# Boundary mask from two digit one-hots, decay matrices in pairs, and the last back turns and statistics placed in the attention loop's first bodies

## The reference, cut to what matters

```python
x = x + jnp.tanh(g_xattn[0]) * _L0_xattn_ref(_layernorm(x, axis=-1), ctx_2048, mask_BxS2_if0, ...)
x = x + jnp.tanh(g_ffn[0]) * _L0_ffn_ref(_layernorm(x, axis=-1), ...)
x = x + jnp.tanh(g_xattn[1]) * _L1_xattn_ref(ctx_2048, _layernorm(x, axis=-1), mask, mask, ...)
x = x + jnp.tanh(g_ffn[1]) * _L1_ffn_ref(_layernorm(x, axis=-1), ...)
```

```python
bidx = jnp.cumsum(patch_lens, axis=1) - 1
boundary_mask = boundary_mask.at[jnp.arange(bsz)[:, None], bidx].set(1)
...
_, s = jax.lax.associative_scan(comb, (a_b, u), axis=1)
plug = jnp.clip(jnp.cumsum(boundary_mask, axis=1) - 1, 0, plen - 1)
depool_out = depool[jnp.arange(bsz)[:, None], plug]
```

## Time and profile before

| | us |
|---|---|
| median of 3 runs | 769.09 (767.45 to 769.4) |
| the profiled execution | 770.5 |
| its span | 768.7 |

### The profile page before, as it was taken

The page is one execution under the profiler, slowest core; times in us unless marked ns, Lnnn a source line. Parts: engine busy times, 40 slices in busy tenths (PEclk is TensorE's granted clock), DMA queues, the critical chain, the costliest instruction groups (busy, mean ns, idle before and its releaser), DMA issues.

```text
span 768.7 us, 12459 instructions
## 1 busy us (share of the span) xinstructions
PE 703.1 (91%) x3826; PEld 491.1 (64%) x3826; DVE 518.5 (67%) x998; ACT 418.9 (54%) x1127; POOL 206.4 (27%) x278
## 2 busy tenths in 40 slices
PE   3788999999999996699999999999999986799996
PEld 1465655554544365588888888888888865456554
DVE  7576477666675376778887877788878787423423
ACT  1666655535545531565566566655665565345352
POOL 3555433310110031533322323233223220212120
PEclk9679999999999998799999999999999999899999
DMA  6621203810000022333334444333344330001112
GB/s 196 219 84 55 83 29 104 234 55 1 0 1 1 0 48 63 83 92 97 82 90 110 110 110 110 81 81 81 86 110 110 82 83 1 1 1 55 35 48 82
DMA packets 46021, 57.48 MB, mean 75 GB/s; under 512 B 14080, under 2 KB 24480, under 8 KB 45856
## 3 DMA queue, kind: packets, MB, share of 16 engines
q1 hardware_dynamic: 45984, 57.03, 27.4%
HBM read 27.52 MB, written 4.19 MB: 41 GB/s over the span
## 4 chain that ended last, share of the span: by engine, by line
PE 77%; ACT 9%; DVE 9%; issue 3%; POOL 0%; DMA 0%; DVEq 0%; ACTq 0%
PE bank L1037 11%; PE bank L1219 7%; ACT c_p L859 7%; PE bank L1292 7%; PE bank L1271 6%; PE bank L1049 5%; PE bank L1411 4%; PE bank L1285 4%; PE bank L1013 4%; PE bank L1258 4%; PE bank L1237 3%; PE bank L1017 3%; DVE c_nmx L1709 3%; PE bank L1402 2%; PE bank L1323 2%
## 5 line engine op out<-in xcount | busy, mean ns | idle before, releaser
L859 ACT ACTIVATE c_p<-bank,c_nmx 128x256 f32<-128x256 f32 x256 | 117.5, 487 | 42.9 <-DVE c_nmx L1709 42.9
L1722 DVE TENSOR_TENSOR c_p<-c_p,c_inv 128x1024 f32<-128x1024 f32 x64 | 91.6, 1432 | 1.1
L1037 PE MATMUL bank<-b_o,cw 128*128 128x512 f32 x192 | 90.8, 603 | 0.0
L1709 DVE TENSOR_REDUCE c_nmx<-bank 128x4 f32<-128x1024 f32 x64 | 75.3, 1219 | 19.9 <-PE bank L1258 19.9
L1271 PE MATMUL bank<-ident,c_p 128*128 128x128 f32 x512 | 65.2, 276 | 8.2 <-ACT c_p L859 8.2
L1271 PEld LDWEIGHTS bank<-ident,c_p 128*128 128x128 f32 x512 | 58.5, 143 | 16.0 <-ACT c_p L859 8.9
L945 ACT ACTIVATE d_h<-bank,b_col 128x512 f32<-128x512 f32 x64 | 39.6, 686 | 45.8 <-PE bank L1403 45.7
L1219 PE MATMUL bank<-c_ctxT,wsrcT 128*128 128x256 f32 x256 | 62.0, 387 | 1.4 <-ACT c_ctxT L835 1.4
L728 ACT ACTIVATE b_h<-bank,cb 128x512 f32<-128x512 f32 x48 | 33.0, 687 | 53.8 <-PE bank L1037 53.7
L1037 PEld LDWEIGHTS bank<-b_o,cw 128*128 128x128 f32 x192 | 34.2, 190 | 41.6 <-issue 41.2
L1729 DVE COPY c_pT<-bank 128x512 f32<-128x512 f32 x64 | 43.9, 686 | 23.8 <-PE bank L1271 23.8
(11 more groups left out here) (185 smaller groups left out, 1450.5 us busy)
## 6 DMA issues: line engine op xcount, KB each, us to landing
c_stack<-c_parts SPq DMA_DIRECT2D x192, 128.0 KB
a_ctx<-in_ctx SPq DMA_DIRECT2D x16, 512.0 KB, 3.4
c_ctx<-in_ctx SPq DMA_DIRECT2D x16, 512.0 KB, 3.5
out_x<-x_sb SPq DMA_DIRECT2D x8, 512.0 KB, 3.0
x_sb<-in_x SPq DMA_DIRECT2D x3, 1024.0 KB, 7.5
mask_b<-in_mask_BxS_fk SPq DMA_DIRECT2D x1, 2048.0 KB, 11.7
x_sb<-in_x SPq DMA_DIRECT2D x2, 512.0 KB, 7.4
wsrc_raw<-in_L_xattn_W_src SPq DMA_DIRECT2D x1, 1024.0 KB, 7.1
```

What stands on the lines that cost most here:

```text
L859: op = nc.scalar.activation(c_p[hg][:, tc, j, :], scores(tc)[:, j, :], ACT.Exp, bias=c_nmx[hg][:, tc, j:j + 1], accum_out=c_sum[hg][:, tc, ...
L1037: op = mm(bank[2 * u + h][:], cw1[:, c, h * P:(h + 1) * P], b_o[n % LANES][:, c, :], start=c == 0, stop=c == DK - 1)
L1709: v.tensor_reduce(c_nmx[hg][:, tc, :], scores(tc), AXIS.X, ALU.max, negate=True)\
L1722: v.tensor_tensor(pr, pr, c_inv[hg][:, :, js].unsqueeze(3).to_broadcast([P, TS, 2, S]), ALU.mult)\
```

## The change

The boundary position is split into a high and a low digit of base 16. Two VectorE instructions compare all 32 columns of positions with 16 digits, 32 small matmuls make, for each batch, a 16 x 16 table of hits, ACT takes its Sign, and 16 small transposes bring the tables back into rows of 256 in bank 1. Lags and decays are made for two batches at a time, over banks 0 to 3 and two `a_z` buffers, in rounds of 2, 1, 2, 2 and 1 pairs; `decay_a` of the last pair comes after the waits for the weights of stage B on ACT. ACT takes the gates and `squares_a(0)` ahead of the Sign and `winT`. At the junction of B and C, `back_b(6)` and `back_b(7)` with `x_b(6)` and `x_b(7)` go from ahead of the loop into body 0; `stats_b(4)` and `stats_b(5)` to the end of body 0, `stats_b(6)` and `stats_b(7)` to the end of body 1; `ones_c(1)` on GpSimd into body 0. `update_b(11, 1)` follows `v_c(0, 3)` at once.

```diff
-LAG_BANK = (1, 2, 3)
-LAGS = (range(0, 3), range(3, 6), range(6, 11), range(11, 16), ())
+LAGS = (range(0, 2), range(2, 3), range(3, 5), range(5, 7), range(7, 8))
+LO = 16
+HI = S // LO
...
-            iota_bf = sb("iota_bf", [P, S], BF16, st)
+            iota_lo = sb("iota_lo", [P, LO], I32, st)
...
-            boundT = sb("boundT", [P, TS, B], F32, st)
-            hit = [sb(f"hit{s}", [P, TS, S], BF16, st) for s in range(4)]
-            row_at = sb("row_at", [P, 2 * B - 1], BF16, st)
-            ends = sb("ends", [B, S], F32, st)
+            bound_i = sb("bound_i", [P, TS * B], I32, st)
+            bound_hi = sb("bound_hi", [P, TS * B], I32, st)
+            bound_lo = sb("bound_lo", [P, TS * B], I32, st)
+            hit_hi = sb("hit_hi", [P, TS * B, HI], BF16, st)
+            hit_lo = sb("hit_lo", [P, TS * B, LO], BF16, st)
...
-            a_z = [sb(f"a_z{s}", [P, QT], F32, st) for s in range(3)]
+            a_z = [sb(f"a_z{s}", [P, 2, QT], F32, st) for s in range(2)]
...
-            a_mT = [sb(f"a_mT{b}", [P, QT], F32, st) for b in range(B)]
+            a_mT = sb("a_mT", [P, B, QT], F32, st)
...
-            nc.gpsimd.iota(iota_bf[:], pattern=[[1, S]], base=0, channel_multiplier=0,
+            nc.gpsimd.iota(iota_lo[:], pattern=[[1, LO]], base=0, channel_multiplier=0,
...
-            nc.gpsimd.memset(row_at[:], 0.0).then_inc(s_zero, 1)
-            pool.wait_ge(s_zero, 2)
-            nc.gpsimd.memset(row_at[:, B - 1:B], 1.0).then_inc(s_const, 1)
...
+                if is_first(b):
+                    pool.wait_ge(c_xb, 2)
+                    ones_c(1, b_x2, NG)
...
+                if isinstance(b, int) and b < 2:
+                    stats_b(NG // 2 + 2 * b)
+                    stats_b(NG // 2 + 2 * b + 1)
...
-            for n in range(NG // 2, NG):
-                stats_b(n)
-            ones_c(1, b_next, 2 * NG)
...
-            act.wait_ge(s_cnt, B)
-            nc.scalar.activation(ends[:], bank[0][0:B, 0:S], ACT.Sign).then_inc(s_end, 1)
-            act.wait_ge(s_wa, 16 * len(loads_a))
-            nc.scalar.activation(gates[:], gates_raw[:], ACT.Tanh).then_inc(s_gate, 1)
-            act.wait_ge(s_winT_ps, 1)
-            for c in range(DK):
-                op = nc.scalar.activation(winT[:, c, :], bank[5][:, c * D:(c + 1) * D], ACT.Copy,
-                                          scale=gres_col[:, c:c + 1])
-            op.then_inc(s_winT, 1)
-
...
-            def decay_a(b):
-                act.wait_ge(a_z_ok, b + 1)
-                nc.scalar.activation(a_mT[b][:], a_z[b % 3][:], ACT.Exp, scale=-DT, bias=lag0_dt[:])                    .then_inc(a_mT_ok, 1)
+            def decay_a(e):
+                act.wait_ge(a_z_ok, e + 1)
+                nc.scalar.activation(a_mT[:, 2 * e:2 * e + 2, :], a_z[e % 2][:], ACT.Exp, scale=-DT, bias=lag0_dt[:])\
+                    .then_inc(a_mT_ok, 1)
...
+            act.wait_ge(s_wa, 16 * len(loads_a))
+            nc.scalar.activation(gates[:], gates_raw[:], ACT.Tanh).then_inc(s_gate, 1)
             squares_a(0)
+            act.wait_ge(s_cnt, 1)
+            nc.scalar.activation(ends[:], bank[0][0:HI, 0:S].rearrange("p (b l) -> p b l", l=LO), ACT.Sign)\
+                .then_inc(s_end, 1)
+            act.wait_ge(s_winT_ps, 1)
+            for c in range(DK):
+                op = nc.scalar.activation(winT[:, c, :], bank[5][:, c * D:(c + 1) * D], ACT.Copy,
+                                          scale=gres_col[:, c:c + 1])
+            op.then_inc(s_winT, 1)
             squares_a(1)
+            scaled_a(0)
             squares_a(2)
-            scaled_a(0)
             scaled_a(1)
             for d in LAGS[0]:
                 decay_a(d)
             turned_a(0)
             for b in range(AHEAD):
                 unit_a(b)
-                for d in LAGS[b + 1]:
-                    decay_a(d)
+                if b < AHEAD - 1:
+                    for d in LAGS[b + 1]:
+                        decay_a(d)
             act.wait_ge(s_wb, 16 * len(loads_b))
             act.wait_ge(s_vconst, 8)
-            act.wait_ge(a_mT_ok, B)
+            for d in LAGS[AHEAD]:
+                decay_a(d)
+            act.wait_ge(a_mT_ok, B // 2)
             turned_b(0)
...
-            pe.wait_ge(s_const, 3)
-
+            pe.wait_ge(s_hit, 1)
             for b in range(B):
-                pe.wait_ge(s_hit, b + 1)
                 for k in range(TS):
-                    op = mm(bank[0][0:B, 0:S], row_at[:, B - 1 - b:2 * B - 1 - b], hit[b % 4][:, k, :],
-                            start=b == 0 and k == 0, stop=b == B - 1 and k == TS - 1)
-                op.then_inc(s_cnt, 1)
+                    op = mm(bank[0][0:HI, b * LO:(b + 1) * LO], hit_hi[:, k * B + b, :], hit_lo[:, k * B + b, :],
+                            start=k == 0, stop=k == TS - 1)
+            op.then_inc(s_cnt, 1)
...
-            def lag_a(b):
-
-                need(pe, a_z_ok, b - 2)
-                mm(bank[LAG_BANK[b % 3]][:, 0:QT], pick[:, b, :], plug[:], start=True, stop=True)\
-                    .then_inc(a_lag_ps, 1)
+            def lag_a(e):
+                need(pe, a_z_ok, e - 1)
+                for i in range(2):
+                    op = mm(banks[:, 2 * (e % 2) + i, 0:QT], pick[:, 2 * e + i, :], plug[:], start=True, stop=True)
+                op.then_inc(a_lag_ps, 1)
...
-                pe.wait_ge(a_mT_ok, b + 1)
+                pe.wait_ge(a_mT_ok, b // 2 + 1)
...
+            pe.wait_ge(s_end, 1)
+            for lo in range(LO):
+                op = nc.tensor.transpose(bank[1][0:B, lo:S:LO], ends[:, :, lo], ident[0:HI, 0:HI])
+            op.then_inc(s_endT, 1)
...
-            pe.wait_ge(a_mT_ok, B)
+            pe.wait_ge(a_mT_ok, B // 2)
...
+                if first:
+                    back_b(NG - 2)
...
+                if first:
+                    back_b(NG - 1)
...
-            back_b(NG - 2)
-            back_b(NG - 1)
             pe.wait_ge(c_vraw, 1)
             pe.wait_ge(b_ok[3], 2 * PAIRS)
-            pe.wait_ge(c_xnTq_ok, 2)
...
-            v.tensor_copy(boundT[:].rearrange("p k b -> p (k b)"), bank[6][:, 0:TS * B]).then_inc(s_boundT, 1)
+            v.tensor_copy(bound_i[:], bank[6][:, 0:TS * B]).then_inc(s_boundT, 1)
             dve.wait_ge(s_boundT, 1)
+            v.tensor_scalar(bound_hi[:], bound_i[:], 4, None, ALU.arith_shift_right)
+            v.tensor_scalar(bound_lo[:], bound_i[:], LO - 1, None, ALU.bitwise_and).then_inc(s_split, 1)
+            dve.wait_ge(s_split, 1)
             dve.wait_ge(s_const, 2)
-
-            def hits(b):
-                need(dve, s_cnt, b - 3)
-                for k in range(TS):
-                    op = v.tensor_scalar(hit[b % 4][:, k, :], iota_bf[:], boundT[:, k, b:b + 1], None, ALU.is_equal)
-                op.then_inc(s_hit, 1)
+            digits = iota_lo[:].unsqueeze(1).to_broadcast([P, TS * B, LO])
+            v.tensor_tensor(hit_hi[:], bound_hi[:].unsqueeze(2).to_broadcast([P, TS * B, HI]), digits, ALU.is_equal)
+            v.tensor_tensor(hit_lo[:], bound_lo[:].unsqueeze(2).to_broadcast([P, TS * B, LO]), digits, ALU.is_equal)\
+                .then_inc(s_hit, 1)
...
-            def lag_a(b):
-
-                dve.wait_ge(a_lag_ps, b + 1)
-                need(dve, a_mT_ok, b - 2)
-                v.tensor_scalar(a_z[b % 3][:].bitcast(I32), bank[LAG_BANK[b % 3]][:, 0:QT].bitcast(I32), FAR, None,
-                                ALU.bitwise_or).then_inc(a_z_ok, 1)
+            def lag_a(e):
+                dve.wait_ge(a_lag_ps, e + 1)
+                need(dve, a_mT_ok, e - 1)
+                v.tensor_scalar(a_z[e % 2][:].bitcast(I32), banks[:, 2 * (e % 2):2 * (e % 2) + 2, 0:QT].bitcast(I32),
+                                FAR, None, ALU.bitwise_or).then_inc(a_z_ok, 1)
...
-            for b in range(8):
-                hits(b)
             moments_a(0)
             moments_a(1)
-            for b in range(8, B):
-                hits(b)
...
-            dve.wait_ge(s_end, 1)
-            v.tensor_tensor_scan(patch[:], ones_row[:], ends[:], -1.0, ALU.mult, ALU.add).then_inc(s_bchain, 1)
+            dve.wait_ge(s_endT, 1)
+            v.tensor_tensor_scan(patch[:], ones_row[:], bank[1][0:B, 0:S], -1.0, ALU.mult, ALU.add).then_inc(s_bchain, 1)
...
+                    v_c(0, 3)
+                    update_b(p - 1, 1)
...
+                if first:
+                    x_b(NG - 2)
...
+                if first:
+                    x_b(NG - 1)
...
+                if isinstance(b, int) and b < 2:
+                    stats_b(NG // 2 + 2 * b)
+                    stats_b(NG // 2 + 2 * b + 1)
...
-            v_c(0, 3)
-            x_b(NG - 2)
-            update_b(PAIRS - 1, 1)
-            x_b(NG - 1)
             biased(c_kT, bank[4], bk_col, 1, c_k_ps, c_k_ok, c_k_split, 2)
-            for n in range(NG // 2, NG):
-                stats_b(n)
```

(18 more changed lines are left out.)

## The result

The changed kernel takes 760.97 us (median of 4 runs, 756.4 to 763.11) against 768.62 for the kernel before: ratio 0.9898, 95% interval 0.987 to 0.9926, so 7.8 us faster, 5.7 to 10. A later set of runs of the same kernel gave 0.992 (0.9891 to 0.9948). The prediction had 765.2 (759 to 770) and "faster" as its likeliest sign: direction and range held, the size was half of what came.

The account below looks back on a forecast made before the run. The prediction took the front as bound by a chain across engines and the attention loop by TensorE. Front 2.7 plus junction 1.2 made 3.9 us, giving 765.2 us against the median, range 759 to 770.

Parts of the forecast that it names:

- The first mixing matmul: Front, TensorE: released by ACT's list, which starts after the gates' DMA; at 22.8 us, 4.1 us earlier.
- `turn_b(0)`: Front: waits for the last decay, behind VectorE's queue; starts at 50.3 instead of 55.69, 5.3 us gross.
- Rival (c): Front: GpSimd stretches VectorE's queue; slower than before from 3.9 us of stretch, 771.7 at 6.5; chance 0.12.
- The clock in the front: Behind TensorE's idle stretch ahead of `turn_b(0)`, work runs at half clock: 1.7 to 3.3 us lost, 2.6 taken.
- the front's gain of +2.7: Front up to `turn_b(0)`: 5.3 us gross, 2.6 taken for clock loss; bounds 0 to +5.3.
- The credit for the pairs: Front, decay matrices for two batches: TensorE no longer waits for z between units; 1.2 of the 5.3 us gross.
- Scores and maxima of batch 0: Junction, body 0: scores need only the stack; scores at 292.8, maxima at 293.6 instead of 308.78.
- The stack of batch 1: Junction: its DMAs wait for `x_b(7)`; scores at 320.3 instead of 328.08, 5 us idle, 2.2 of clock loss.
- Statistics 6 and 7: End of body 1, ahead of body 2's maxima: 3.2 us arrive on TensorE, plus 1.2 of clock loss.
- Junction in all: Between stages B and C: 5.6 us gained, less 3.2 and 1.2, gives +1.2; bounds -2 to +6.
- Rival (b): Front gains nothing, or the junction's gains are eaten in body 2: about 768 us; chance 0.20.
- Rival (a): The clock holds behind the new front and junction waits: 6.0 us of loss returned, 759.2, half 762; chance 0.18.

Follow-up runs that it names:

- front alone: Changed kernel's front (mask, ACT's order, decay matrices in pairs) with the junction of the kernel before: 763.5 us, ratio 0.9932.
- filler run: Changed kernel with 44 idle identity transposes on TensorE in the 5.9 us wait ahead of `turn_b(0)`: 759.87 us, ratio 0.9872.
- Three comparisons: Kernels without decay pairs over the same with pairs: 0.9964 and 0.9960 with the junction changed, 0.9990 with the junction of before.
- the last kernel: Changed kernel with fourth lag pair one unit earlier, statistics in VectorE's gaps, `x_b(7)` early and VectorE's body 0 list reordered: 745.56 us, ratio 0.9693.

## Why the prediction held, and where it was off

**The first mixing matmul**: 22.8 forecast, 22.06 measured, by the chain named: the gates' DMA, then ACT's list. ACT started at 13.07 instead of 12.65, and its list took 1.0 us less than before (13.07 to 22.01, against 16.94 to 26.86), where I had taken it as the same. The hits were ready at 9.57, near the late end of the span given for them (10.3): one VectorE instruction of 32 elements took 3.00 us beside GpSimd's `pick` (below). The 32 small matmuls took 0.96 us in all, where I had bounds of 1.6 and 4.9, and the 16 transposes 0.60, where I took 2.1. None of it reached ACT.

**`turn_b(0)`**: 50.3 forecast, 49.94 measured; the wait of about 5 us is 5.90, and its releaser is the last decay, behind VectorE's queue, as argued. That it fits to 0.4 us is in part luck: VectorE's list started at 27.96 instead of 29.1, since unit 0 came earlier and ran partly at the full clock, and took 20.7 us instead of 20.0. Two z of 768 elements take 1.79 or one 0.92, against the 0.85 to 0.88 taken. Rival (c) happened only in small: beside the GpSimd adds a copy of 64 x 128 elements took 1.30 us (0.21 in the kernel before) and one pair of operands 1.06 (0.85), 1.3 us of stretch, where by the forecast's sum 3.9 would have made the change a loss. The updates of `finish_a` took 0.74 to 0.75 each.

**The clock in the front**: 2.6 us of loss forecast. `turn_b(0)` came 5.75 us earlier, the second layer 3.44 us earlier (60.02 in the trace before, 56.58 after), so 2.3 were lost. The term that was mis-sized is the front's gain of +2.7: the sum ended there, and took no account of the waits that follow. The next turn comes 4.05 us earlier than 64.31 (60.26; the normalisation in front of it took 1.68 us, not the 2.30 of the earlier trace rows), and in the profiled run the clock then held at 63.57. The next group of the second layer is 5.7 us ahead of before, 66.59 against 72.33 there, and 5.2 in the second trace. The timed front alone is 5.2 (3.5 to 6.9). The filler run is the other side of this: which of the waits between 45 and 65 us the clock falls behind differs from kernel to kernel and from run to run, and a sum that charges one of them and lets the others stand as before was wrong by 2.5 us here.

**The credit for the pairs**: the prediction gave them 1.2 of the 5.3 gross and took 2.6 of clock off; net -1.4. Three comparisons have them between -0.8 and -3.1, none clear of the noise. The sign agrees, and it was hidden in the sum: stated by itself it would have said that this part of the change does not pay.

**Scores and maxima of batch 0**: 292.8 and 293.6 forecast in the time of before; 292.50 and 293.24 measured (286.77 and 287.51, with the 5.73 that the front gives). Right.

**Back turns**: 1.97 each taken from the earlier trace rows, 1.04 measured. The row of before stood behind a wait of 4.80 us and was itself at half clock; I copied a duration without asking at which clock it had run. It cost little, as `b_x2` was complete at 308.24 in that time against 309.0.

**The stack of batch 1**: this is the junction's mis-sized term. I had the scores 11.6 us behind the first of the stack's DMAs, from the earlier trace rows; the trace has 9.8 from the first DMA at 302.54 to the scores at 312.35. In the earlier trace rows PE had its own work between, so the distance there was not the stack's. The scores came at 318.08 in the time of before (320.3 forecast), and the wait was 3.39 us, not 5. Clock loss behind it: 1.73 (3.00 + 2.51 less 2 x 1.89), against 2.2; 0.7 of it is made good by the scores of batch 2, and there the gain is 9.0 (349.93 less 335.23 less 5.73) instead of 5.6. In the second trace of the changed kernel the wait is 3.27 us, and q and v behind it take 1.89 each: no clock loss at all.

**Statistics 6 and 7**: 3.2 + 1.2 = 4.4 off. From the scores of batch 2 to those of batch 3 it is 26.84 us in the first trace (335.23 to 362.07) and 25.87 in the second, against 21.94 before (349.93 to 371.87): they give back 4.9 and 3.9. That leaves the junction 4.07 in the first trace (9.80 in all less the front's 5.73). Moving the statistics brought 5.5 or more by the ratios. The mechanism and the size were right. Junction in all: 1.2 forecast, 3.4 (2.2 to 4.6) timed.

Rival (b) is out, since both parts kept a gain. Rival (a) is half of what happened. Its half value, 762, is nearer to the measured 761 than the forecast is. In the first trace all three clock losses are in the rows, but the first was made good at the next group; in the second the one behind the stack is missing. The forecast had the waits right and charged the clock for each of them in full, and not all of it stayed.

## What to carry to other kernels

Before a duration is moved to another place, ask what stood before it: behind a wait the row may be at half clock, and the distance between a DMA and its reader may hold the reader's own work. When a queue is reordered, count the whole list ahead of which a small job could have stood; the job inherits all of it (3.4 us of VectorE's list, 4.35 at `turn_b(0)`, for jobs of 0.9). Bookkeeping with a late deadline belongs into its engine's own waits, not at the end of a loop body, where it stands ahead of the next body's first maxima. And before a small edit is priced by one trace, take a second of the same kernel: here two of them differed by 3.6 us at `turn_b(0)`.

## What the runs showed of the hardware

**A small VectorE instruction stuck beside GpSimd.** GpSimd's row for `pick` in the changed kernel is

```profile
4.52 3.60 POOL L551 TENSOR_TENSOR pick<-pick_col,pick_row 18x2048 bf16<-18x2048 f32 x1
```

and `bound_hi`, 32 elements, started at 5.16 and lasted 3.00 us, to its end; `bound_lo`, of the same shape, took 0.17. The kernel before paid the same: its 16 hits beside `pick` took 6.34 us, and the same work again, with GpSimd idle,

```profile
13.27 3.19 DVE L1473 TENSOR_SCALAR hit<-iota_bf,boundT 128x256 bf16<-128x256 bf16 x16
```

Similarly `xn_c(2)` took 2.18 us at 293.64 beside two GpSimd instructions (293.11 to 295.68), but 0.73 in the last kernel, where it runs ahead of them. The Trainium skill (SBUF — State Buffer, Who interferes with whom) says that a VectorE instruction in a two-port mode, which a tensor_scalar can be in, and a GpSimd instruction lock each other out of their shared port, and that whoever issues first keeps it for the whole instruction. These rows agree, if `bound_hi`, the hits and `xn_c` run in such a mode, which no row shows. In the sum, 3.00 us hung on nothing here, since ACT waited for a DMA.

**The clock differs between executions of one kernel.** The runs of the kernel before lay from 767.1 to 770.5 in the first two sets; those of the changed kernel spread over more, 756.4 to 763.1, with mean granted clocks of 0.974 to 0.982. Where a kernel has waits behind which the clock sometimes falls, one profile is a sample: the second profiled run of the changed kernel had its second layer at 54.84, the first at 56.58, and behind like waits for the stack (3.27 and 3.39 us) q took 1.89 in the one and 3.00 in the other.
